# A window-attention block and a deformable convolution on one core: attention's scores and outputs ahead of a slot's sample matmuls, the rare path as a loop of nine passes, turned samples copied by ScalarE

## The chip, the cores and the metric

The kernel runs on one core of a Trainium2 chip. The metric is the device time of one execution in microseconds (us). Everything is computed in float32. The engines are TensorE (PE in the profile; PEld is its weight load), VectorE (DVE), ScalarE (ACT), GpSimd (POOL) and SyncE (SP), which issues nearly all transfers. Each engine takes its instructions strictly in program order and waits on semaphores.

## The reference, cut to what matters

The input is `x`, 16 images of 128 channels and 56x56 pixels. Layer 0 is a block with window attention, layer 1 a modulated deformable 3x3 convolution (8 groups of 16 channels, 9 taps, so 72 samples for each pixel) of one of a few upsampled maps.

```
x = x + dwconv3x3(x, pos_w, pos_b)
y = layernorm(x); q, k, v = y @ qkv_w + qkv_b           # 49 windows of 8x8 pixels
idx = top_k(mean(q) . mean(k), 4)                       # 4 windows of keys for each window
o = softmax(q . k[idx] * SCALE) @ v[idx]                # 4 heads of 32
x = x + (o + dwconv5x5(v, lepe_w)) @ wo_w + wo_b
x = x + gelu(layernorm(x) @ mlp_w1 + mlp_b1) @ mlp_w2 + mlp_b2
...
g = 1 + sigmoid(relu(w_atten . mean(x)))
f = relu(w_off . concat(relu(w_fsm . (x * g)), 2 * feat_up))
off, mask = conv3x3(f, w_offmask) + b_offmask           # 72 dy, 72 dx, 72 mask logits
val = bilinear(feat_up, position + off) * sigmoid(mask) # 4 corners for each of 72 samples
out = relu(w_dcn . val + b_dcn) + x
```

## The kernel before

**Two images at once.** The main loop is software pipelined over images. While layer 0 of image i is computed (`xi` in the code, by the functions `x_slot`, `x_first`, `x_rest`), layer 1 of image i-1 is computed as well (`di`). One round has NT = 28 tiles of two output rows, and each tile has Q = 9 slots, so a round has 252 slots, numbered n = 9 t + q. Fifteen rounds work on two images; before them stands a round with layer 0 alone, and after them one with layer 1 alone. What a slot issues on each engine is written out by hand in the `body` function of that engine; there is no scheduler.

**Layer 1 in a slot.** `windows` (L1025) is 32 small PE matmuls that interpolate eight samples for each pixel along x, from the map piece `fx` and the hat functions `hats`, into one of two PSUM tensors `windows0/1`. `weigh` (L1573) on DVE multiplies the result by the row weights. PE may write slot n only when `weigh` of slot n-2 is done (semaphore `window_weighted`). POOL adds the rows in `add_rows` (L687, L689, L692). In slots q = 5, 6, 7, 8 and 0 PE also turns one or two blocks of finished samples of the tile before (`turn_samples`, L999) into spare columns of the same PSUM tensor, and `copy_samples` (L1562, on DVE right behind `weigh`) copies them to `valt`, 128x256, in q = 0 128x128. `windows` of slot n+2 waits for that copy as well. `deform` (L1036, 9 matmuls, q = 5) consumes `valt`; ScalarE's `relu` (L1279) reads its result. `offsets` (L983, 9 matmuls) stands in q = 0, `turn_columns` (L988) in q = 2, `sum_outside` (L993) in q = 3.

**Attention in slots.** Each of the 49 windows of pixels w has its steps one slot apart, and a new window starts every three slots, from slot A0 = 59 on: slot 0 `scores` on PE (L902); slot 1 `maxes` on DVE (L1489) and `exps` on ACT (L1183); slot 2 `turn` on PE (L911), at the slot's end; slot 3 `copy_turned` on ACT (L1190); slot 4 `pv` on PE (L926); slot 5 `scale_heads` on DVE (L1494, L1496). There are two score banks, so `scores` of window w waits for `scale_heads` of window w-2, which DVE does one slot earlier (semaphore `heads_scaled`). Since 59 leaves 5 when divided by 9, `scores` always stands in q = 2, 5, 8, `pv` in q = 0, 3, 6, and `turn` and `scale_heads` in q = 1, 4, 7. Attention takes slots 59 to 210.

**The 5x5 convolution** on v (`lepe`, L1507 and L1510) is 25 DVE operations for each of seven bands, two or three in each of the 12 slots before a band's end; between them lie 9 slots with the band's output projection and its two-layer network (`post`, steps k = 0 to 8; the Gelu with its table loads is step 7 on ACT, the last matmul step 8 on PE, L956). In the first 27 slots DVE does the 3x3 convolution instead (L1460).

**The rare path.** `general` on POOL runs once a tile, tests a flag and branches over the code at L708 when no sample of the tile lies outside the rows that the fast path holds. Otherwise it recomputes the tile's samples: nine passes, written out one after the other, of 32 gathers (L759), a wait, and four additions and products. In this data one tile of 448 takes it.

The order on PE within a slot is in `body` of the PE program:

```
if di is not None:
    windows(di, t, q)
    ... turn_samples(bi, bt, p, hb[n % 2])
if xi is not None:
    x_first(xi, n)          # pv, then scores
```

behind which come `offsets`, `turn_columns`, `sum_outside`, `deform` and `x_rest` (the projections, `post`, and last `turn`).

Of the kernel before, what the change touches and what calls it, by code (L numbers as in the profile page):

```python
# [8 lines left out]
U32 = mybir.dt.uint32  # L9
ALU = mybir.AluOpType  # L10
ACT = mybir.ActivationFunctionType
# [3 lines left out]
NIMG = B  # L15
# [135 lines left out]
def build(nc, a, out):  # L151
# [9 lines left out]
    with ExitStack() as ctx:  # L161
# [93 lines left out]
        gix = sb("gix", [128, S, 2, 2], U32)  # L255
        gw = sb("gw", [128, S, 2, 2])
        gbuf = sb("gbuf", [128, 8, 2, 2, CG])

        s_w = sem("weights_loaded")
        s_src = sem("small_maps_loaded")  # L260
# [402 lines left out]
        def _(pool):  # L663
# [38 lines left out]
            def general(i, t):  # L702
# [5 lines left out]
                with pool.If(f > 0):  # L708
# [43 lines left out]
                    pool.drain()  # L752
                    pool.tensor_tensor(gw[:, :, 1], gw[:, :, 1], lx, ALU.mult)
                    pool.drain()
                    for n in range(S // 8):
                        for s in range(8):
                            for x in range(2):
                                for y in range(2):
                                    pool.indirect_dma_start(  # L759
                                        gbuf[:, s, x, y], None, fmap,  # L760
                                        bass.IndirectOffsetOnAxis(ap=gix[:, 8 * n + s, x, y:y + 1], axis=0)
                                    ).then_inc(s_fb, 16)
                        pool.wait_ge(s_fb, 32 * 16)
                        hold(pool, "pool")
                        pool.inc_swdge_sem([s_fb], [32 * 16], mode="sub")
                        g = gbuf[:].rearrange("p s x y c -> p (s x y) c")
                        pool.tensor_tensor(g, g, gw[:, 8 * n:8 * n + 8].rearrange("p s x y -> p (s x y)").unsqueeze(2)
                                           .to_broadcast([128, 32, CG]), ALU.mult)
                        pool.drain()
                        pool.tensor_tensor(gbuf[:, :, 0], gbuf[:, :, 0], gbuf[:, :, 1], ALU.add)  # L770
                        pool.drain()
                        pool.tensor_tensor(val[t % 2][:, 8 * n * CG:8 * (n + 1) * CG].rearrange("p (s c) -> p s c", c=CG),
                                           gbuf[:, :, 0, 0], gbuf[:, :, 0, 1], ALU.add)
                        pool.drain()
                pool.drain().then_inc(s_vok, 1)  # L775

# [35 lines left out]
        def _(pe):  # L812
# [254 lines left out]
            def body(xi, di):  # L1067
                for t in range(NT):
                    fi, ft = tile_of(di, xi, t + 2)
                    pi, pt_ = before(di, t, 2)  # L1070
                    for q in range(Q):
                        n = t * Q + q
                        if di is not None:
                            windows(di, t, q)
                            bi, bt, p = pair_of(di, t, q)
                            if bi is not None:
                                turn_samples(bi, bt, p, hb[n % 2])
                        if xi is not None:
                            x_first(xi, n)
                        if fi is not None and q == OM:  # L1080
                            offsets(fi, ft)
                        if fi is not None and q == PXT:
                            turn_columns(fi, ft)
                        if fi is not None and q == PXT + 1:
                            sum_outside(fi, ft)
                        if pi is not None and q == WD:
                            deform(pi, pt_)
                        if xi is not None:
                            x_rest(xi, n)
# [16 lines left out]
        def _(act):  # L1106
# [164 lines left out]
            def row_hats(i, t):  # L1271
                v = wy[t % 2][:].rearrange("p s r -> p (s r)")
                act.wait_ge(s_rab, cnt(i, NT, t + 1))
                act.activation(v, v, ACT.Relu, scale=-1.0, bias=1.0).then_inc(s_wh, 1)

            def relu(i, t):
                act.wait_ge(s_do, cnt(i, NT, t + 1))
                wait(act, s_fin, cnt(i, NT, t - 1))
                act.activation(rt[t % 2][:], bm[:, 216:344], ACT.Relu, bias=col(BD)).then_inc(s_rt, 1)  # L1279
# [22 lines left out]
            def body(xi, di):  # L1302
                for t in range(NT):
                    ni, nt = tile_of(di, xi, t + 1)
                    fi, ft = tile_of(di, xi, t + 2)
                    pi, pt_ = before(di, t, 2)
                    for q in range(Q):
                        hi, hg = group_of(di, xi, t * NG + q // CPG + 1)
                        if hi is not None:
                            column_distances(hi, hg, q % CPG)  # L1310
                        if fi is not None and q == PXT - 1:
                            outside(fi, ft)
                        if fi is not None and q == PXT:
                            copy_columns(fi, ft)
                        if ni is not None and q == WYH:
                            row_sizes(ni, nt)
                        if fi is not None and q == PXT + 1:
                            masks(fi, ft, 0)
                        if pi is not None and q == WD:
                            relu(pi, pt_)  # L1320
                        if ni is not None and q == WYH:
                            row_hats(ni, nt)
                        if fi is not None and q == PXT - 1:
                            outside_sum(fi, ft)
                        if xi is not None:
                            x_slot(xi, t * Q + q)
                        if fi is not None and q in (PXT + 1, PXT + 2):
                            masks(fi, ft, q - PXT)
                        if hi is not None:
                            column_hats(hi, hg, q % CPG)  # L1330
# [4 lines left out]
            with act.Fori(2, NIMG) as i:  # L1335
                body((i, 0), (i, -1))
            body(None, NIMG - 1)
            for t in range(NT - 2, NT):
                relu(NIMG - 1, t)

        @block.vector
        def _(dve):
# [214 lines left out]
            def copy_samples(i, t, p, bank):  # L1557

                dve.wait_ge(s_vt, cnt(i, NP * NT, NP * t + p + 1))
                wait(dve, s_do, cnt(i, NT, t - 1))  # L1560
                k = min(2, KK - 2 * p)
                dve.tensor_copy(valt[t % 2][:, 2 * p:2 * p + k, :], bank[:, 0:k, SPARE:SPARE + 128]).then_inc(s_ve, 1)  # L1562
# [31 lines left out]
            def body(xi, di):  # L1594
                for t in range(NT):
                    fi, ft = tile_of(di, xi, t + 2)
                    for q in range(Q):
# [3 lines left out]
                        if di is not None:  # L1601
                            bi, bt, p = pair_of(di, t, q)
                            if bi is not None:
                                dve.wait_ge(s_vt, cnt(bi, NP * NT, NP * bt + p + 1))
                            weigh(di, t, q)
                            if bi is not None:
                                copy_samples(bi, bt, p, hb[n % 2])
                        if xi is not None:
                            w = step_of(n, 5)
                            if w is not None:  # L1610
# [14 lines left out]
            for t, p in LAST_PAIRS:  # L1625
                copy_samples(NIMG - 1, t, p, hb[p % 2])


# [36 lines left out]
```

## Time and profile before

| | |
|---|---|
| median of three runs | 13466.48 us (13452.15 to 13472.7) |
| profiled execution, its own time | 13485.3 us |
| its span, first to last instruction | 13483.5 us |
| PE busy / weight load busy | 10597.7 us (79%) / 7976.9 us (59%) |
| DVE busy | 8469.6 us (63%) |
| ACT busy | 8472.9 us (63%) |
| POOL busy | 6730.6 us (50%) |
| mean granted PE clock | 0.916 of full speed |

No engine is busy all the time. Set-up takes some 270 us and the first round, with layer 0 alone, ends near 837 us, where the first `weigh` starts. Then the rounds are even. A busy time in the table mixes stretches in which different engines set the pace, so the order of work inside a slot has to be read from the timeline.

### The profile page before, as it was taken

To read this page: it belongs to the slowest core of one execution; us is meant where nothing else is said; L and a number is where in the kernel's file an instruction comes from. 1 tells how busy PE (TensorE), PEld (TensorE's weight loads), DVE (VectorE), ACT (ScalarE), POOL (GpSimd) and SP (SyncE) were. 2 spreads that over 40 slices of the span, in tenths; PEclk is the share of its full clock that TensorE was granted. 3 is DMA by queue.
4 is the path that set the end of the run, shared out by engine and by line. 5 is a ranking of instruction groups with operands and counts; after the bars stand their busy time and mean duration, and the time that the engine had idled before them with its cause. 6 is when DMAs were issued, how large, how long until landed. Compare 5 with 4: busy or idle time off the path is not lost.

```text
span 13483.5 us, 498781 instructions
## 1 busy us (share of the span) xinstructions
PE 10597.7 (79%) x187900; PEld 7976.9 (59%) x187900; DVE 8469.6 (63%) x13829; ACT 8472.9 (63%) x17364; POOL 6730.6 (50%) x6167
## 2 busy tenths in 40 slices
PE   3678888888888888888888888888888888832888
PEld 2346666666666666666666666666666666622666
DVE  6456666666766666676666766666666766622654
ACT  1346666666666666666666666666666666632676
POOL 0034554545455554545455454545545454566467
PEclk8779999999999999999999999999999999976998
DMA  4234454544444454544445454444444444421454
GB/s 130 56 85 121 115 123 116 121 112 121 120 113 122 118 120 109 122 119 115 120 119 121 111 122 118 116 120 121 119 113 121 117 117 121 117 63 39 111 129 109
DMA packets 1847031, 1516.80 MB, mean 112 GB/s; under 512 B 1006688, under 2 KB 1381984, under 8 KB 1841568
## 3 DMA queue, kind: packets, MB, share of 16 engines
q1 hardware_dynamic: 1834468, 1474.31, 44.0%
q8 instruction: 1549, 25.38, 0.8%
q14 instruction: 1798, 14.73, 0.4%
q0 software_dynamic: 9216, 2.38, 0.2%
HBM read 1297.68 MB, written 178.25 MB: 109 GB/s over the span
## 4 chain that ended last, share of the span: by engine, by line
issue 43%; POOLq 25%; PE 11%; POOL 9%; DVE 3%; ACT 3%; DVEq 2%; SPq 2%; DMA 1%; ACTq 0%
POOLq L688 14%; POOLq L690 8%; POOL gbuf L759 2%; POOL wy L679 2%; PE windows L1025 2%; PE bank_small L983 2%; PE bank_small L1036 2%; POOL val L692 1%; POOL xb L699 1%; DVE bank_post L1510 1%; POOLq L705 1%; POOL prod L687 1%; POOL pxy L668 1%; PE bank_scores L902 1%; PE windows L999 1%
## 5 line engine op out<-in xcount | busy, mean ns | idle before, releaser
L1573 DVE TENSOR_TENSOR prod<-windows,wy 128x640 f32<-128x640 f32 x4032 | 3302.2, 821 | 2803.9 <-PE windows L999 1967.4
L687 POOL TENSOR_TENSOR prod<-prod 128x768 f32<-128x768 f32 x1344 | 2452.3, 1825 | 3743.8 <-DVE prod L1573 3736.9
L1025 PEld LDWEIGHTS windows<-fx,hats 64*64 64x64 f32 x129024 | 2629.4, 137 | 1561.6 <-issue 1477.8
L1025 PE MATMUL windows<-fx,hats 64*64 64x80 f32 x129024 | 3278.2, 241 | 341.6 <-issue 118.6
L1234 ACT ACTIVATE hats<-hats,cst 128x512 f32<-128x512 f32 x4032 | 2868.0, 711 | 93.7 <-DMA hats<-sample_columns 59.4
L1238 ACT ACTIVATE hats<-hats 128x512 f32<-128x512 f32 x4032 | 2511.7, 623 | 21.3
L1510 DVE SCALAR_TENSOR_TENSOR bank_post<-xpad,lepw,bank_post 128x448 f32<-128x448 f32 x2688 | 1851.0, 689 | 231.4 <-issue 13.2
L983 PE MATMUL bank_small<-wom,ofp 128*128 128x216 f32 x8064 | 1636.6, 359 | 0.0
L689 POOL TENSOR_TENSOR prod<-prod 128x384 f32<-128x384 f32 x1344 | 1470.7, 1094 | 198.0 <-issue 7.1
L983 PEld LDWEIGHTS bank_small<-wom,ofp 128*128 128x128 f32 x8064 | 1513.3, 199 | 33.4 <-issue 2.7
L692 POOL TENSOR_TENSOR val<-prod 128x384 f32<-128x384 f32 x1344 | 1386.2, 1031 | 269.6 <-issue 230.9
L1183 ACT ACTIVATE pr<-bank_scores,nmx 128x256 f32<-128x256 f32 x1568 | 655.8, 469 | 1267.2 <-DVE nmx L1489 1267.0
L668 POOL TENSOR_SCALAR pxy<-pxy 128x72 f32<-128x72 f32 x448 | 176.6, 394 | 2295.5 <-issue 1388.2
L902 PE MATMUL bank_scores<-ksel,qbd 128*128 128x256 f32 x3136 | 944.7, 428 | 354.8 <-DVE ob L1496 254.2
L911 PE MATMUL bank_scores<-cst,pr 128*128 128x128 f32 x3136 | 532.8, 296 | 861.4 <-ACT pr L1183 861.2
L1036 PE MATMUL bank_small<-valt,wdcn 128*128 128x128 f32 x8064 | 1081.5, 294 | 38.7 <-DVE flag L1555 36.7
L1036 PEld LDWEIGHTS bank_small<-valt,wdcn 128*128 128x128 f32 x8064 | 1066.5, 210 | 63.7 <-issue 42.6
L911 PEld LDWEIGHTS bank_scores<-cst,pr 128*128 128x128 f32 x3136 | 379.7, 149 | 1100.6 <-ACT pr L1183 938.5
L999 PE MATMUL windows<-cst,val 128*128 128x128 f32 x4032 | 961.8, 312 | 45.8 <-POOLq L775 42.1
L902 PEld LDWEIGHTS bank_scores<-ksel,qbd 128*128 128x128 f32 x3136 | 592.1, 210 | 491.7 <-issue 427.5
L1562 DVE COPY valt<-windows 128x256 f32<-128x256 f32 (+1 forms) x2240 | 867.3, 387 | 11.0 <-PE windows L999 11.0
L1279 ACT ACTIVATE rt<-bank_small,cols 128x128 f32<-128x128 f32 x448 | 163.9, 366 | 1127.7 <-PE bank_small L1036 1127.6
(193 smaller groups left out, 12943.8 us busy)
## 6 DMA issues: line engine op xcount, KB each, us to landing
hats<-sample_columns SPq DMA_DIRECT2D x2688, 336.0 KB
ksel<-k_windows SPq DMA_DIRECT2D x3136, 32.0 KB
vsel<-v_windows SPq DMA_DIRECT2D x3136, 32.0 KB
fx<-map_columns SPq DMA_DIRECT2D x64, 420.0 KB
xpad<-in_x SPq DMA_DIRECT2D x17, 1568.0 KB, 11.4
q_windows<-qb SPq DMA_DIRECT2D x112, 224.0 KB, 2.7
k_windows<-kb SPq DMA_DIRECT2D x112, 224.0 KB, 3.0
v_windows<-vb SPq DMA_DIRECT2D x112, 224.0 KB, 3.2
```

The source lines that it names most:

```text
L687: pool.tensor_tensor(v[:, :, 0:n], v[:, :, 0:n], v[:, :, n:2 * n], ALU.add)
L688: pool.drain()
L689: pool.tensor_tensor(v[:, :, 0], v[:, :, 0], v[:, :, 1], ALU.add)
L692: pool.tensor_tensor(val[t % 2][:, g * GS * CG:(g + 1) * GS * CG].rearrange("p (s c) -> p s c", c=CG), v[:, :, 0], v[:, :, 2 if n == 3 els ...
L902: mm = pe.matmul(bank_of(w)[:, h * 256:(h + 1) * 256], qbd[:, j, 2 * h:2 * h + 2, :].rearrange("p h q -> p (h q)"), ksel[s][:], start=True ...
L983: mm = pe.matmul(bm[:, 0:3 * S], ofp[:, at:at + TP], wom[:, k, :], start=(k == 0), stop=(k == KK - 1))
L1025: last[h] = pe.matmul(o[m], hat[:, m], fx[XP * h:XP * h + XP, g, row:row + WR, :].rearrange("p r c -> p (r c)"), start=True, stop=True)
L1036: mm = pe.matmul(bm[:, 216:344], wdcn[:, k, :], valt[t % 2][:, k, :], start=(k == 0), stop=(k == KK - 1))
L1234: act.activation(chunk(n, c), chunk(n, c), ACT.Abs, bias=const("xneg")).then_inc(s_cab, 1)
L1238: act.activation(chunk(n, c), chunk(n, c), ACT.Relu, scale=-1.0, bias=1.0).then_inc(s_hat, 1)
L1510: dve.scalar_tensor_tensor(out=olv, in0=v, scalar=lepw[:, k:k + 1], in1=olv, op0=ALU.mult, op1=ALU.add)
L1573: dve.tensor_tensor(o, x, w.unsqueeze(3).to_broadcast([128, 2, CP * WR, CG]), ALU.mult).then_inc(s_wm, 1)
```

## The change

There are three edits. First, in the PE program `x_first` (that is `pv` and `scores`) moves from behind `windows` and `turn_samples` of the slot to ahead of them. Second, `copy_samples` moves from DVE to ACT: there it stands behind ACT's attention and projection work of the slot and ahead of `column_hats`, and it waits for `weigh` of its slot (`window_weighted`). Third, the nine passes of the rare path become a loop: each pass first copies its indices and weights to the fixed tensors `gin` and `gwn`, and its sum goes to `gsum` and from there to `val`.

```
-                    for n in range(S // 8):
+                    with pool.Fori(0, S // 8) as n:
+                        pool.tensor_copy(gin..., gix...[:, bass.ds(n * 32, 32)])
+                        pool.tensor_copy(gwn..., gw...[:, bass.ds(n * 32, 32)])
+                        pool.drain()
...
-                                        bass.IndirectOffsetOnAxis(ap=gix[:, 8 * n + s, x, y:y + 1], axis=0)
+                                        bass.IndirectOffsetOnAxis(ap=gin[:, s, x, y:y + 1], axis=0)
...
-                        pool.tensor_tensor(val[t % 2][...], gbuf[:, :, 0, 0], gbuf[:, :, 0, 1], ALU.add)
+                        pool.tensor_tensor(gsum[:], gbuf[:, :, 0, 0], gbuf[:, :, 0, 1], ALU.add)
+                        pool.drain()
+                        pool.tensor_copy(val[t % 2][:, bass.ds(n * (8 * CG), 8 * CG)], gsum...)
...
+                        if xi is not None:
+                            x_first(xi, n)
                         if di is not None:
                             windows(di, t, q)
                             bi, bt, p = pair_of(di, t, q)
                             if bi is not None:
                                 turn_samples(bi, bt, p, hb[n % 2])
-                        if xi is not None:
-                            x_first(xi, n)
...
+            def copy_samples(i, t, p, bank):
+                act.wait_ge(s_vt, cnt(i, NP * NT, NP * t + p + 1))
+                wait(act, s_do, cnt(i, NT, t - 1))
+                k = min(2, KK - 2 * p)
+                act.activation(valt[t % 2][:, 2 * p:2 * p + k, :], bank[:, 0:k, SPARE:SPARE + 128],
+                               ACT.Copy).then_inc(s_ve, 1)
...
                         if xi is not None:
                             x_slot(xi, t * Q + q)
+                        if bi is not None:
+                            act.wait_ge(s_wm, cnt(di, NT * Q, t * Q + q + 1))
+                            copy_samples(bi, bt, p, hb[(t * Q + q) % 2])
...
                             weigh(di, t, q)
-                            if bi is not None:
-                                copy_samples(bi, bt, p, hb[n % 2])
```

On PE, in a tile of the attention stretch, slots q = 5 and 6 stand like this in the kernel before (L1025 is `windows`, L999 `turn_samples`, L902 `scores`, L1036 `deform`, L926 `pv`):

```order
L1025 MATMUL windows<-fx,hats 64x80 x16
L999 MATMUL windows<-cst,val 128x128 x2
L902 MATMUL bank_scores<-ksel,qbd 128x256 x2
L1036 MATMUL bank_small<-valt,wdcn 128x128 x9
L1025 MATMUL windows<-fx,hats 64x80 x16
L999 MATMUL windows<-cst,val 128x128 x2
L926 MATMUL bank_scores<-pt,vsel 32x64 x8
L926 MATMUL bank_scores<-pt,cst 32x64 x8
```

The same two slots on PE in the changed kernel, whose line numbers differ (L1036 is now `windows`, L1010 `turn_samples`, L913 `scores`, L1047 `deform`, L937 `pv`):

```order
L913 MATMUL bank_scores<-ksel,qbd 128x256 x2
L1036 MATMUL windows<-fx,hats 64x80 x16
L1010 MATMUL windows<-cst,val 128x128 x2
L1047 MATMUL bank_small<-valt,wdcn 128x128 x9
L937 MATMUL bank_scores<-pt,vsel 32x64 x8
L937 MATMUL bank_scores<-pt,cst 32x64 x8
L1036 MATMUL windows<-fx,hats 64x80 x16
L1010 MATMUL windows<-cst,val 128x128 x2
```

`scores` now stands ahead of the first `windows`, and `pv` between `deform` and the second.

On ACT, the same two slots in the changed kernel (L1298 is `relu`, L1201 `copy_turned`, L1292 the new copy, L1249 and L1245 the hats, L1194 `exps`); in the kernel before the two rows of L1292 are not there and the rest stands the same:

```order
L1298 ACTIVATE rt<-bank_small,cols 128x128 [waits tile_finished,deform_matmul]
L1201 ACTIVATE pt<-bank_scores 128x512 [waits pv_ready,probs_turned]
L1292 ACTIVATE valt<-windows 128x256 [waits deform_matmul,samples_turned,window_weighted]
L1249 ACTIVATE hats<-hats 128x512 [waits column_distances_ready]
L1245 ACTIVATE hats<-hats,cst 128x512 [waits columns_spread0]
L1194 ACTIVATE pr<-bank_scores,nmx 128x256 [waits probs_turned,max_ready]
L1194 ACTIVATE pr<-bank_scores,nmx 128x256
L1292 ACTIVATE valt<-windows 128x256 [waits deform_matmul,samples_turned,window_weighted]
```

`copy_turned`, which `pv` needs, stands behind `relu`, which needs `deform`, in both kernels.

## Rows read from the trace of the kernel before

**Rows 1.** Busy by stretch, ten rounds: us, PE, PEld, DVE, ACT, POOL, clock, DMA.
```profile
3957.00:11759.00 7802.00, 6489.64 (x117080) 4910.62 (x117080) 5174.97 (x8561) 5252.39 (x10800) 4030.32 (x3640) 0.94 0.48 118
```

**Rows 2.** Waits, same stretch: waiter, line, whom; total us, times, longest.
```profile
PE bank_scores L911 <- ACT pr L1183: 270.9, 211, 4.5
PE bank_scores L926 <- ACT pt L1190: 166.7, 160, 1.4
PE bank_scores L902 <- DVE ob L1496: 155.6, 230, 1.2
...
DVE prod L1573 <- PE windows L999: 944.7, 668, 11.1
DVE prod L1573 <- PE windows L1025: 473.2, 505, 3.6
```

**Rows 3.** PE's timeline, slots q = 5 to 8: start, us, line, [idle before].
```profile
6583.25 1.10 PE L902 MATMUL bank_scores<-ksel,qbd 128*128 128x256 f32 x4
6584.19 2.17 PE L1036 MATMUL bank_small<-valt,wdcn 128*128 128x128 f32 x18
6586.29 0.78 PE L1025 MATMUL windows<-fx,hats 64*64 64x80 f32 x32
6587.00 0.44 PE L999 MATMUL windows<-cst,val 128*128 128x128 f32 x2
6587.39 0.43 PE L926 MATMUL bank_scores<-pt,vsel 128*32 128x64 f32 x16
...
6592.92 1.10 PE L902 MATMUL bank_scores<-ksel,qbd 128*128 128x256 f32 x4 [0.85 <-DVE ob L1496]
```

**Rows 4.** DVE's timeline, slots q = 7 and 8 of that tile.
```profile
6590.86 0.82 DVE L1573 TENSOR_TENSOR prod<-windows,wy 128x640 f32<-128x640 f32 x1
6591.59 0.41 DVE L1562 COPY valt<-windows 128x256 f32<-128x256 f32 x1
6591.92 0.55 DVE L1494 RECIPROCAL rinv<-bank_scores 128x64 f32<-128x64 f32 x1
6592.55 0.22 DVE L1496 TENSOR_TENSOR ob<-bank_scores,rinv 128x64 f32<-128x64 f32 x1
6592.86 1.45 DVE L1510 SCALAR_TENSOR_TENSOR bank_post<-xpad,lepw,bank_post 128x448 f32<-128x448 f32 x2
6594.23 0.82 DVE L1573 TENSOR_TENSOR prod<-windows,wy 128x640 f32<-128x640 f32 x1
```

**Rows 5.** ACT's timeline, that tile: slot q = 2, then slot q = 5.
```profile
6577.49 0.27 ACT L1243 ACTIVATE pxs<-bank_small 72x128 f32<-72x128 f32 x1 [0.58 <-PE bank_small L988]
6577.80 0.50 ACT L1269 ACTIVATE wy<-wy 128x360 f32<-128x360 f32 x1
...
6578.74 0.58 ACT L1190 ACTIVATE pt<-bank_scores 128x512 f32<-128x512 f32 x1
...
6586.40 0.37 ACT L1279 ACTIVATE rt<-bank_small,cols 128x128 f32<-128x128 f32 x1 [2.50 <-PE bank_small L1036]
6586.66 0.59 ACT L1190 ACTIVATE pt<-bank_scores 128x512 f32<-128x512 f32 x1
```

**Rows 6.** The page's costliest groups: busy us, mean ns, idle before, releaser.
```profile
L1562 DVE COPY valt<-windows 128x256 f32<-128x256 f32 (+1 forms) x2240 | 867.3, 387 | 11.0 <-PE windows L999 11.0
L1183 ACT ACTIVATE pr<-bank_scores,nmx 128x256 f32<-128x256 f32 x1568 | 655.8, 469 | 1267.2 <-DVE nmx L1489 1267.0
```

**Rows 7.** PE's timeline, step 8 of `post`, and the clock of its stretch.
```profile
6638.00 4.84 PE L956 MATMUL bank_post<-hid,w 128*128 128x448 f32 x6 [3.75 <-ACT hid L1208]
6638.00:6642.80 4.80, 4.80 (x7) 2.23 (x8) 0.00 (x0) 3.93 (x7) 0.00 (x0) 0.50 0.58 135
```

**Rows 8.** POOL, whole span: the gathers, and the first operation behind the branch.
```profile
L759 POOL DMA_INDIRECT gbuf<-map_columns,gix x288 | 272.2, 945 | 92.2 <-issue 92.2
L668 POOL TENSOR_SCALAR pxy<-pxy 128x72 f32<-128x72 f32 x448 | 176.6, 394 | 2295.5 <-issue 1388.2
```

More of the change, by code:

```diff
@@ L257, in build @@
         gbuf = sb("gbuf", [128, 8, 2, 2, CG])
+        gin = sb("gin", [128, 8, 2, 2], U32)
+        gwn = sb("gwn", [128, 8, 2, 2])
+        gsum = sb("gsum", [128, 8, CG])
         s_w = sem("weights_loaded")
@@ L754, in general @@
                     pool.drain()
-                    for n in range(S // 8):
+                    with pool.Fori(0, S // 8) as n:
+                        pool.tensor_copy(gin[:].rearrange("p s x y -> p (s x y)"),
+                                         gix[:].rearrange("p s x y -> p (s x y)")[:, bass.ds(n * 32, 32)])
+                        pool.tensor_copy(gwn[:].rearrange("p s x y -> p (s x y)"),
+                                         gw[:].rearrange("p s x y -> p (s x y)")[:, bass.ds(n * 32, 32)])
+                        pool.drain()
                         for s in range(8):
@@ L766, in general @@
                         g = gbuf[:].rearrange("p s x y c -> p (s x y) c")
-                        pool.tensor_tensor(g, g, gw[:, 8 * n:8 * n + 8].rearrange("p s x y -> p (s x y)").unsqueeze(2)
+                        pool.tensor_tensor(g, g, gwn[:].rearrange("p s x y -> p (s x y)").unsqueeze(2)
                                            .to_broadcast([128, 32, CG]), ALU.mult)
@@ L771, in general @@
                         pool.drain()
-                        pool.tensor_tensor(val[t % 2][:, 8 * n * CG:8 * (n + 1) * CG].rearrange("p (s c) -> p s c", c=CG),
-                                           gbuf[:, :, 0, 0], gbuf[:, :, 0, 1], ALU.add)
+                        pool.tensor_tensor(gsum[:], gbuf[:, :, 0, 0], gbuf[:, :, 0, 1], ALU.add)
+                        pool.drain()
+                        pool.tensor_copy(val[t % 2][:, bass.ds(n * (8 * CG), 8 * CG)],
+                                         gsum[:].rearrange("p s c -> p (s c)"))
                         pool.drain()
@@ L1326, in body @@
                             x_slot(xi, t * Q + q)
+                        bi, bt, p = pair_of(di, t, q) if di is not None else (None, None, None)
+                        if bi is not None:
+                            act.wait_ge(s_wm, cnt(di, NT * Q, t * Q + q + 1))
+                            copy_samples(bi, bt, p, hb[(t * Q + q) % 2])
                         if fi is not None and q in (PXT + 1, PXT + 2):
@@ L1337, in _ @@
             body(None, NIMG - 1)
-            for t in range(NT - 2, NT):
-                relu(NIMG - 1, t)
+            for t, p in LAST_PAIRS:
+                copy_samples(NIMG - 1, t, p, hb[p % 2])
+                if p == NP - 1:
+                    relu(NIMG - 1, t)
         @block.vector
@@ L1555, in flags @@
                 dve.tensor_scalar(flag[0:1, t % 4:t % 4 + 1], bm[0:1, 472:473], 0.0, None, ALU.is_gt).then_inc(s_fl, 1)
[L1557 to L1562, printed above, removed]
             def weigh(i, t, q):
@@ L1624, in _ @@
             body(None, NIMG - 1)
-            for t, p in LAST_PAIRS:
-                copy_samples(NIMG - 1, t, p, hb[p % 2])
 def kernel(**inputs):
```

## The prediction

> **What bounds the kernel now.** I read the busy table by stretch first, then the waits, then the timelines of one tile. The ten even rounds take 780.2 us each, PE is busy for 83% of them, DVE for 66%, ACT for 67% and POOL for 52% [rows 1], so no engine alone is the bound: they hand work to each other. The waits say how. DVE waits before `weigh` for PE's sample matmuls, 142 us a round, and PE waits for ACT and DVE before the three attention steps: 27 us a round before `turn`, 17 before `pv`, 16 before `scores` [rows 2]. These waits are short and frequent, so what stands behind each of them in PE's order matters.
>
> The timelines show a tile of a stretch in which DVE also has taps of the 5x5 convolution. There DVE has no gap from `weigh` of q = 7 to `weigh` of q = 8: product 0.73 from start to start, copy 0.33, reciprocal and scaling 0.85 to the result, two taps 1.37 to the next product [rows 4]. PE was a slot ahead: `scores` of q = 8 started 0.15 us after the scaling ended, and it had waited 0.85 us for it [rows 3, 4], with `windows` of q = 8 already done. That order, samples first and attention's waits second, is what lets DVE go on. In this stretch DVE is the bound.
>
> **Part 1, the copy leaves DVE.** It costs DVE 0.33 us in a slot with two blocks [rows 4] and an estimated 0.20 in q = 0, so 1.5 us a tile of nine slots. On ACT I take 0.42 us for it: `exps` reads the same 128x256 from PSUM in 0.47, and DVE's mean is 0.39 [rows 6]. ACT is busy for two thirds, and `column_hats` behind the copy is made three slots ahead, so this lies beside other work. It adds a wait: ACT stands until `weigh` of the slot is done; behind it are the hats and then `copy_turned`. `windows` two slots later waits for the copy as before, with about a slot to spare. Alone this part would gain up to 1.5 us a tile where DVE is the bound.
>
> **Part 2, `pv` and `scores` ahead of the samples.** Here I follow one tile with taps in the new order. Lengths: `scores` 0.94 from start to start, `windows` 0.71 and then the turned samples 0.44 to their end, `deform` 2.10 [rows 3]; `pv` 0.50 (two halves, estimated from the 0.43 of each and their overlap); a signal between engines about 0.08 (an estimate between the 0.04 from `deform`'s end, at 6586.36, to `relu` and the 0.15 above) [rows 3, 5].
> (a) *q = 2, 5, 8.* Count from the end of scaling in the slot before. Now `scores` must run before `windows`: 0.08 + 0.94 + 0.78 + 0.08 = 1.88 us until `weigh` may start, and in q = 5 and 8, with turned samples, 0.08 + 0.94 + 0.71 + 0.44 + 0.08 = 2.25. DVE has only its taps to do, 0.09 + 1.37 = 1.46. It stalls 0.4 + 0.8 + 0.8 = 2.0 us a tile where it stalled for nothing.
> (b) *q = 6.* `pv` needs `copy_turned`, which stands on ACT behind `relu`, which needs `deform` of q = 5 [rows 3, 5]. Before, `windows` of q = 6 ran in that time: it began at 6586.29, `relu` at 6586.40, the copy at 6586.66, `pv` at 6587.39. Now from the start of `weigh` of q = 5: `deform`, begun about 0.2 before, ends at +1.95, `relu` lets the copy start at +2.27, which ends at +2.86, `pv` runs from +2.94 for 0.50, `windows` and samples end at +4.59, `weigh` may start at +4.67. DVE is ready at 0.74 + 1.46 = 2.20, so it stalls 2.5 us.
> (c) *q = 3.* `copy_turned` stands behind the copy of the turned columns, which needs L988 behind `windows` of q = 2, and behind two operations on the row weights; from 6577.49 to its start is 1.25 us, and it takes 0.58 [rows 5]. From the start of `weigh` of q = 2: +0.2 for L988, +1.25, +0.58, +0.08, `pv` 0.50, `windows` 0.78, signal 0.08: 3.4 against DVE's 2.2, a stall of 1.2 us.
> The three stalls make 5.7 us. Less the 1.5 us of part 1 and about 0.2 that DVE stalls there now, a tile with taps becomes 4.0 us longer. The taps stand in 7 x 12 = 84 of the 152 attention slots, 9.3 tiles: +37 us a round.
> In the other 68 slots (7.6 tiles) DVE has slack, but the chain through PE has the same three waits ahead of `windows`. From below, 0: they lie beside what `post` makes PE wait for anyway. From above, 4.0 as with taps. I take 2.7, nearer the upper end, since (b) and (c) are waits of PE itself and don't depend on taps: +20 us a round. In slots 0 to 58 `x_first` is empty; DVE does the 3x3 convolution in 27 of them and I count three tiles of part 1, -4 us.
> A round gains 37 + 20 - 4 = 53 us, fifteen rounds 800 us.
>
> **Part 3, the loop in the rare path.** It runs once, and all engines stand meanwhile. Its 288 gathers take (272.2 + 92.2) / 288 = 1.27 us each [rows 8] in either form. Each pass adds two copies of 32 numbers, one of 128 and two drains; I take 1.3 us, so 12 in all, between 5 and 20. Eight jumps back: the nearest row is the branch over the code, behind which POOL stands 1388.2 / 448 = 3.1 us on the mean [rows 8]; bounds 0 and 6, taken 2.6, so 21 us. The sum is +33, from +5 to +70. The branch over the path now skips about a ninth of the code. That may shorten those 3.1 us, but POOL waits for DVE's products anyway, and I count nothing. The Trainium skill (Runtime: NRT & Kernel Launch, Instruction fetch mechanics) speaks against the loop: a taken branch to code that is not at hand forces a fetch, and unrolled code is preferred. By it the eight jumps cost like the one over the code, 8 x 3.1 = 25 us; it changes the sum by 4 us.
>
> **Sum.** 13485.3 + 800 + 33 = 14318 us for the profiled execution. This lies 19 us above the median of the runs, so the median of the changed kernel should be near 14300 us, 6% slower.
>
> **The rivals.**
> *The copy decides.* If PE, freed from waits by an earlier `pv`, stayed a slot ahead, stalls (a) to (c) would not form, and only part 1 would be left: 1.5 us in 9.3 + 3 tiles, 18 us a round, 15 x 18 = 277 us less, plus 33: 13220. For it: DVE has no gap in the tile with taps, so each operation that leaves counts. Against it: `scores` was seen to wait for the scaling 230 times in 490, though it stood behind `windows` [rows 2]. It decides from the point where the scaling ends more than 2 us before `windows` is due. Chance 8%.
> *The delays are half absorbed.* PE's stalls may merge with waits it has now, which are 780.2 - 649.0 = 131 us a round in all [rows 1]. Then 27 us a round: 13467 + 400 + 33 = 13900. Chance 18%.
> *The clock falls.* After 3.75 us without a matmul in step 8 of `post`, the granted clock was 0.50 (1.2 GHz) and six matmuls took 4.84 us [rows 7]. New gaps of 1 to 2 us could lower it elsewhere. If it were lower by 0.05 of 0.94 [rows 1], the 649 us that PE is busy in a round would grow by 5%, 34 us, fifteen times: 500 more, 14800. Against it: the four matmuls of `scores` took 1.10 us behind a gap of 0.85 as they did behind none [rows 3]. The Trainium skill (TensorE: Matmul & The Clock Gate, HAM oscillation) has this as a rule: idle gaps between bursts make the clock fall again and again. The rows agree for the long gap and not for the short ones. Chance 15%.
> *It cancels.* Stalls and the copy's gain meet within 0.2%, 13440 to 13493. Chance 3%.
>
> **How the numbers follow.** The forecast has 56%. The 2.7 us of the slots without taps, taken from 0 to 4, alone move it by 15 x 7.6 x 2.7 = 308 down and 148 up, to 13990 and 14450; the loop's bounds move it by 28 down and 37 up. The range reaches into the absorbed and the clock case: 13800 to 14700. A measurement of this kernel tells about 0.2% from no change. Faster by more than that: 0.08; within: 0.03; slower: 0.89.
>
> **What would show it.** Right: in rounds of about 833 us, PE's wait before `pv` for L1201 and before `scores` for the scaling grow to several times their 17 and 16 us, DVE's wait before `weigh` for `windows` grows from 142 us by about 50, DVE is busy 867.3 / 16 = 54 us a round less [rows 6] and ACT as much more; before `windows` of q = 6 stands `pv`, which waited about 1 us for `copy_turned`; the rare path takes some 30 us longer. Wrong: if `weigh` of q = 6 starts within 3 us of that of q = 5, (b) is false; if rounds without attention waits are longer too, it is ACT's new wait that delays the hats; if PE's mean clock is under 0.90 in the rounds, the clock case holds.

## The result, and the profile after

| | before | after |
|---|---|---|
| median | 13465.69 us (4 runs) | 14665.61 us (14653.94 to 14686.4, 4 runs) |
| ratio | | 1.089, 95% interval 1.0875 to 1.0913 |
| span of the profiled execution | 13483.5 us | 14660.6 us |
| mean granted PE clock | 0.916 | 0.894 |
| PE, DVE, ACT, POOL busy | 79, 63, 63, 50% | 75, 54, 61, 46% |

The changed kernel is 1200 us or 8.9% slower. The forecast was 14300 us, with a range from 13800 to 14700.

In the kernel after, line numbers are shifted: `windows` is L1036, `turn_samples` L1010, `scores` L913, `turn` L922, `pv` L937, `deform` L1047, the copy L1292 on ACT, `weigh` L1592. First, ten rounds by the busy table (us, then PE, PEld, DVE, ACT, POOL, clock, DMA share, GB/s), to be read against [rows 1], and the waits of the same stretch against [rows 2]:

```profile
3406.00:12032.00 8626.00, 6748.88 (x117082) 5027.82 (x117081) 4807.03 (x7161) 5587.76 (x12201) 4039.96 (x3640) 0.91 0.43 106
```

```profile
PE bank_scores L937 <- ACT pt L1201: 445.1, 350, 1.9
PE bank_scores L913 <- DVE ob L1522: 389.6, 312, 1.6
PE bank_scores L922 <- ACT pr L1194: 298.6, 210, 1.6
...
DVE prod L1592 <- PE windows L1010: 1841.6, 936, 10.5
DVE prod L1592 <- PE windows L1036: 788.9, 679, 3.7
```

A round takes 862.6 us instead of 780.2, 82.4 more. It splits in two: PE is busy 674.9 us instead of 649.0, with the same number of matmuls, which is 25.9 us of slower matmuls; and PE is idle 187.7 us instead of 131.2, which is 56.5 us of waits. Where the trace has the clock at 0.50, PE is busy for 78.2 us of a round before and for 130.1 after. At full speed the 51.9 us more would have been half as long, so 26.0 us of busy time come from the clock, which is the whole growth. PE's waits before `pv` and `scores` grew from 17 and 16 to 45 and 39 us a round, and DVE's wait before `weigh` from 142 to 263.

The tile with taps, on PE (start, us, engine, line, names, [idle before]); it answers to [rows 3]:

```profile
7250.20 1.10 PE L913 MATMUL bank_scores<-ksel,qbd 128*128 128x256 f32 x4 [1.24 <-DVE ob L1522]
...
7254.18 0.43 PE L937 MATMUL bank_scores<-pt,vsel 128*32 128x64 f32 x16 [1.93 <-ACT pt L1201]
...
7258.05 1.12 PE L922 MATMUL bank_scores<-cst,pr 128*128 128x128 f32 x4 [1.03 <-ACT pr L1194]
7260.31 2.04 PE L913 MATMUL bank_scores<-ksel,qbd 128*128 128x256 f32 x4 [1.14 <-DVE ob L1522]
7262.28 1.34 PE L1036 MATMUL windows<-fx,hats 64*64 64x80 f32 x32
7263.56 0.69 PE L1010 MATMUL windows<-cst,val 128*128 128x128 f32 x2
7264.04 2.91 PE L1047 MATMUL bank_small<-valt,wdcn 128*128 128x128 f32 x18
7267.99 0.43 PE L937 MATMUL bank_scores<-pt,vsel 128*32 128x64 f32 x16 [1.04 <-ACT pt L1201]
```

And `weigh` on DVE in the slots q = 2 to 8 of that tile, of which [rows 4] show q = 7 and 8 before:

```profile
7252.11 0.82 DVE L1592 TENSOR_TENSOR prod<-windows,wy 128x640 f32<-128x640 f32 x1 [0.52 <-PE windows L1036]
...
7255.70 0.82 DVE L1592 TENSOR_TENSOR prod<-windows,wy 128x640 f32<-128x640 f32 x1 [1.22 <-PE windows L1036]
...
7258.58 0.82 DVE L1592 TENSOR_TENSOR prod<-windows,wy 128x640 f32<-128x640 f32 x1
...
7264.37 0.83 DVE L1592 TENSOR_TENSOR prod<-windows,wy 128x640 f32<-128x640 f32 x1 [2.62 <-PE windows L1010]
...
7269.94 0.82 DVE L1592 TENSOR_TENSOR prod<-windows,wy 128x640 f32<-128x640 f32 x1 [3.20 <-PE windows L1010]
...
7272.81 0.82 DVE L1592 TENSOR_TENSOR prod<-windows,wy 128x640 f32<-128x640 f32 x1
...
7278.61 0.82 DVE L1592 TENSOR_TENSOR prod<-windows,wy 128x640 f32<-128x640 f32 x1 [1.91 <-PE windows L1010]
```

DVE has a gap wherever the prediction put one: before q = 2, 3, 5, 6 and 8. Together they are 9.5 us, where the prediction had 5.7. `scores` of q = 5 takes 2.04 us where it took 1.10, `windows` 1.34 for 0.78, the turned samples 0.69 for 0.44. The busy table says why, with the clock in the third column from the right:

```profile
7252.20:7254.20 2.00, 0.07 (x4) 0.05 (x5) 1.83 (x3) 1.82 (x5) 1.18 (x1) 1.00 0.22 49
...
7255.60:7256.90 1.30, 1.30 (x36) 1.14 (x34) 1.20 (x2) 0.00 (x0) 1.10 (x2) 0.50 0.98 258
...
7260.20:7264.70 4.50, 4.39 (x42) 3.42 (x43) 1.72 (x4) 0.36 (x1) 0.00 (x0) 0.50 0.14 37
...
7266.00:7267.00 1.00, 0.95 (x9) 0.76 (x7) 0.69 (x1) 0.01 (x1) 1.00 (x1) 1.00 0.86 279
...
7272.20:7273.30 1.10, 1.02 (x4) 0.65 (x4) 1.09 (x2) 1.10 (x4) 0.00 (x0) 0.59 0.23 58
```

The clock fell to its lower level, 1.2 GHz, soon after PE had waited 1.24 us before `scores` of q = 2 and 1.93 us before `pv` of q = 3, with 2.05 us of matmuls between the two waits. It stayed there through the next two waits, 1.03 and 1.14 us, and came back during the 2.91 us of `deform`.

On POOL, the gathers and the first operation behind the branch, to be read against [rows 8] (the second from the answer by lines):

```profile
L768 POOL DMA_INDIRECT gbuf<-map_columns,gin x288: 938/944/1189, 13104.1 to 13511.4; - x144
L672 POOL TENSOR_SCALAR pxy<-pxy 128x72 f32<-128x72 f32 x448 | 198.8, 444 | 1081.0 <-DVE pxy L1577 930.4 <-issue 150.6
```

From the branch to the end of the rare path it is 417.4 us before and 428.9 after. The idle time put down to issue behind the branch fell from 1388.2 to 150.6 us. From the branch to the next instruction it was 2.8 us at the median of the 448 times before, and 0.4 after.

### The profile page after: what moved, and what is told of

It is laid out like the page before. It is cut to its first block, busy times and chain, and to the rows that moved or that the text cites. A ratio compares the mean times of both kernels' runs of the same rounds, so it can differ in the third digit from the quotient of the medians.

```text
span 14660.6 us, 500856 instructions
## 1 busy us (share of the span) xinstructions
PE 10958.6 (75%) x187900; PEld 8130.5 (55%) x187900; DVE 7870.5 (54%) x11589; ACT 8998.4 (61%) x19604; POOL 6754.0 (46%) x6194
## 4 chain that ended last, share of the span: by engine, by line
PE 39%; issue 23%; DVEq 9%; POOLq 8%; DVE 8%; ACT 8%; POOL 4%; ACTq 1%; DMA 1%; SPq 1%
PE windows L1036 10%; PE bank_small L994 6%; POOLq L692 4%; PE bank_small L1047 4%; PE bank_scores L913 4%; DVEq L1485 3%; PE windows L1010 3%; DVEq L1521 3%; POOLq L694 2%; PE bank_scores L937 2%; PE bank_post L967 2%; DVE bank_post L1536 2%; DVEq L1535 2%; POOL gbuf L768 2%; DVE prod L1592 2%
## 5 line engine op out<-in xcount | busy, mean ns | idle before, releaser
L1592 DVE TENSOR_TENSOR prod<-windows,wy 128x640 f32<-128x640 f32 x4032 | 3306.5, 822 | 4578.4 <-PE windows L1010 3305.9
L1036 PE MATMUL windows<-fx,hats 64*64 64x80 f32 x129024 | 3433.9, 249 | 317.7 <-ACT valt L1292 154.0
L1036 PEld LDWEIGHTS windows<-fx,hats 64*64 64x64 f32 x129024 | 2768.5, 144 | 1543.8 <-issue 1440.5
L1245 ACT ACTIVATE hats<-hats,cst 128x512 f32<-128x512 f32 x4032 | 2885.2, 716 | 41.7 <-issue 41.7
L1249 ACT ACTIVATE hats<-hats 128x512 f32<-128x512 f32 x4032 | 2521.1, 625 | 0.5
L913 PE MATMUL bank_scores<-ksel,qbd 128*128 128x256 f32 x3136 | 1056.0, 469 | 731.0 <-DVE ob L1522 603.5
L696 POOL TENSOR_TENSOR val<-prod 128x384 f32<-128x384 f32 x1344 | 1445.3, 1075 | 268.3 <-issue 237.6
L1194 ACT ACTIVATE pr<-bank_scores,nmx 128x256 f32<-128x256 f32 x1568 | 657.0, 470 | 1337.1 <-DVE nmx L1515 1337.1
L1292 ACT ACTIVATE valt<-windows 128x256 f32<-128x256 f32 (+1 forms) x2240 | 806.3, 360 | 742.5 <-DVE prod L1592 694.8
L922 PE MATMUL bank_scores<-cst,pr 128*128 128x128 f32 x3136 | 539.9, 299 | 915.7 <-ACT pr L1194 915.7
L913 PEld LDWEIGHTS bank_scores<-ksel,qbd 128*128 128x128 f32 x3136 | 629.4, 222 | 934.5 <-issue 868.5
L1298 ACT ACTIVATE rt<-bank_small,cols 128x128 f32<-128x128 f32 x448 | 163.7, 365 | 1479.3 <-PE bank_small L1047 1479.2
L1047 PE MATMUL bank_small<-valt,wdcn 128*128 128x128 f32 x8064 | 1044.0, 287 | 32.6 <-DVE flag L1581 31.8
L1047 PEld LDWEIGHTS bank_small<-valt,wdcn 128*128 128x128 f32 x8064 | 1011.6, 204 | 47.3 <-issue 45.0
L922 PEld LDWEIGHTS bank_scores<-cst,pr 128*128 128x128 f32 x3136 | 381.2, 150 | 1139.7 <-ACT pr L1194 991.4
L1010 PE MATMUL windows<-cst,val 128*128 128x128 f32 x4032 | 997.8, 323 | 4.2 <-issue 1.6
L937 PE MATMUL bank_scores<-pt,vsel 128*32 128x64 f32 x12544 | 367.6, 239 | 668.3 <-ACT pt L1201 668.3
```

What stands on the lines that cost most here:

```text
L696: pool.tensor_tensor(val[t % 2][:, g * GS * CG:(g + 1) * GS * CG].rearrange("p (s c) -> p s c", c=CG), v[:, :, 0], v[:, :, 2 if n == 3 els ...
L913: mm = pe.matmul(bank_of(w)[:, h * 256:(h + 1) * 256], qbd[:, j, 2 * h:2 * h + 2, :].rearrange("p h q -> p (h q)"), ksel[s][:], start=True ...
L1010: mm = pe.transpose(bank[:, k % 2, SPARE:SPARE + 128], val[t % 2][:, k * 128:(k + 1) * 128], ident)
L1036: last[h] = pe.matmul(o[m], hat[:, m], fx[XP * h:XP * h + XP, g, row:row + WR, :].rearrange("p r c -> p (r c)"), start=True, stop=True)
L1047: mm = pe.matmul(bm[:, 216:344], wdcn[:, k, :], valt[t % 2][:, k, :], start=(k == 0), stop=(k == KK - 1))
L1245: act.activation(chunk(n, c), chunk(n, c), ACT.Abs, bias=const("xneg")).then_inc(s_cab, 1)
```

## The experiments

All ratios are against runs of the kernel before on the same chip. In the code cuts, what stands behind # is a note of this text.

**e1_order: the first edit alone.**

```
+                        if xi is not None:
+                            x_first(xi, n)
                         if di is not None:
                             windows(di, t, q)
...
-                        if xi is not None:
-                            x_first(xi, n)
```

> Only the first edit: pv and scores ahead of the sample matmuls on PE; the copy stays on DVE, the rare path stays unrolled. Theory 'order' (PE's sample matmuls now stand behind attention's waits, and that is the whole loss): at least as slow as the changed kernel, 14650 to 15000 us, since DVE also keeps the 1.5 us of copies a tile. Rival 'ScalarE' (the new wait of ScalarE for weigh delays hats and copies, the order costs little): within 150 us of the kernel before, 13450 to 13600.

Measured: 15041.16 us, ratio 1.117 (1.1155 to 1.1193). Ten of its rounds:

```profile
3479.00:12317.00 8838.00, 6857.43 (x117082) 5123.41 (x117081) 5214.87 (x8561) 5252.42 (x10800) 4020.47 (x3640) 0.90 0.42 104
```

It loses 1572 us, more than the whole change and a little more than its theory's upper end of 15000. 'ScalarE' falls: nothing of the loss needs the copy on ACT. A round is 103.6 us longer: 198.1 us idle (66.9 more) and 685.7 busy (36.8 more).

**e2_copy: the second edit alone.**

```
+                        if bi is not None:
+                            act.wait_ge(s_wm, cnt(di, NT * Q, t * Q + q + 1))
+                            copy_samples(bi, bt, p, hb[(t * Q + q) % 2])      # ScalarE
...
                             weigh(di, t, q)
-                            if bi is not None:
-                                copy_samples(bi, bt, p, hb[n % 2])            # VectorE
```

> Only the second edit: copy_samples on ScalarE. Theory 'order': faster than before by 100 to 280 us, 13190 to 13370, since DVE is relieved of 1.5 us a tile where it sets the pace. Rival 'ScalarE': slower by several hundred us, 14000 and more. The changed kernel's last round (layer 1 alone) was 49 us shorter than before; if that comes from the copy, it is seen here too, if it comes from the shorter branch over the rare path, it is not.

Measured: 13330.4 us, ratio 0.990 (0.9887 to 0.9921), 139 us faster. The copies on ACT and what they wait for:

```profile
L1281 ACT ACTIVATE valt<-windows 128x256 f32<-128x256 f32 (+1 forms) x2240 | 806.7, 360 | 468.5 <-DVE prod L1581 411.0 <-PE windows L999 54.3
```

ACT stands 411 us for `weigh` in the whole kernel, and the kernel is faster all the same: the rounds are 771 us. From the first to the last `weigh` of the last round (layer 1 alone) the kernel before takes 514.7 us, the changed kernel 465.2 and this one 504.2, so most of what the changed kernel saved there is not the copy's.

**e3_loop: the third edit alone.**

```
-                    for n in range(S // 8):
+                    with pool.Fori(0, S // 8) as n:
...
```

> Only the third edit: the rare path as a loop. The changed kernel's trace has the rare path at 428.9 us from branch to end against 417.4, and the branch over it at 0.4 against 2.8 us. If PowerL's branch is covered by waits: 13465 + 12 = 13477 us. If it is exposed in the last round (28 tiles of 2.4 us) and at tile starts: 50 to 100 us less than before, 13370 to 13420.

('PowerL' is a slip for POOL.) Measured: 13385.99 us, ratio 0.994 (0.992 to 0.9963), 83 us faster. POOL's first operation behind the branch:

```profile
L672 POOL TENSOR_SCALAR pxy<-pxy 128x72 f32<-128x72 f32 x448 | 190.2, 425 | 1147.6 <-DVE pxy L1562 1043.5 <-issue 91.9 <-DVE flag L1566 12.2
```

The last round takes 456.2 us instead of 514.7, 58 less, and the others 2.5 less at the median. In the last round of the kernel before, the branch is seen to be exposed; its waits there:

```profile
POOL pxy L668 <- issue: 92.3, 25, 5.2
...
ACT pxy L1258 <- POOL pxy L668: 42.7, 19, 3.4
...
DVE prod L1573 <- POOL val L692: 38.1, 25, 3.1
...
PE windows L999 <- POOLq L775: 27.0, 16, 2.5
```

POOL's late `samples_checked` holds PE's `turn_samples`, and its late masks and sums hold DVE. The sum is right: 58 in the last round and 14 times 2.5 in the others, less the 11.5 that the rare path takes longer, make 82. In rounds with attention so little of the branch is left; that it lies beside other waits there is argued, not tried.

**e4_scores and e5_pv: the first edit in two halves.** In the first, only `scores` goes ahead of `windows`, in the second only `pv`.

> The kernel before with scores alone ahead of windows; pv stays behind it. Stall (a) of the prediction alone: 2.0 us a tile in 16.9 tiles is 34 us a round, 13980 us; with matmuls at the 1.2 GHz level behind the longer gap up to 60 us a round, 14370. Rival (the whole loss sits with pv, scores cost nothing): 13420 to 13520.

> The kernel before with pv alone ahead of windows; scores stay behind it. Stalls (b) and (c): 3.7 us a tile in 16.9 tiles is 62 us a round, 14400 us; between 14200 and 14700. Rival (the loss sits with scores): 13420 to 13600. If the two halves are independent, their losses add up to the 1572 us of both.

Measured: 14273.9 us, ratio 1.060 (1.0578 to 1.0627) for `scores`, and 14294.51 us, ratio 1.062 (1.0595 to 1.0638) for `pv`. Ten rounds of each, and the wait that each step has:

```profile
3335.00:11664.00 8329.00, 6718.51 (x117084) 5008.17 (x117083) 5215.79 (x8561) 5254.44 (x10801) 4024.51 (x3642) 0.92 0.44 110
PE bank_scores L902 <- DVE ob L1500: 481.9, 385, 2.0
PE bank_scores L926 <- ACT pt L1194: 166.8, 160, 1.4
```

```profile
3334.00:11677.00 8343.00, 6690.94 (x117083) 5077.45 (x117082) 5186.54 (x8561) 5251.27 (x10801) 4032.73 (x3641) 0.91 0.44 110
PE bank_scores L926 <- ACT pt L1194: 432.7, 343, 2.1
PE bank_scores L902 <- DVE ob L1500: 128.4, 203, 1.2
```

Each half lengthens its own wait and not the other's, which stays (166.8 us for 166.7) or gets a little shorter (128.4 for 155.6). The losses of 799 and 820 us add up to 1619, those of both together were 1572: they are nearly independent. The loss with `scores` ahead lies between the 13980 of the stall alone and the 14370 with slow matmuls, as forecast. A round is 52.7 us longer with `scores` ahead and 54.1 with `pv`: idle time grew by 29.8 and 34.0 us, busy time by 22.9 and 20.1. Against the forecast idle time, 34 for (a) fits, and 62 for (b) and (c) was nearly double of what is seen.

**e6_filler and e9_filler4: does the clock matter?** Both are the changed kernel with small matmuls ahead of every `pv` and `scores`; their results aren't used. They wait for what `windows` of the slot waits for, so `pv` and `scores` behind them now do as well, which is a second change beside the filled gap.

```
+                    for _ in range(8):        # 4 in e9_filler4
+                        pe.matmul(hb[(t * Q + q) % 2][:, 0, 448:512], ident, const("ident")[:, 0:64],
+                                  start=True, stop=True)
...
+                        if xi is not None and di is not None and (
+                                step_of(n, 4) is not None or step_of(n, 0) is not None):
+                            filler(di, t, q)  # waits for what windows(di, t, q) waits for
                         if xi is not None:
                             x_first(xi, n)
```

> The changed kernel with eight small matmuls (128x128 weights, 64 columns, about 0.8 us in all) on PE ahead of every pv and every scores, into spare columns of the PSUM tensor that the slot's samples will go to; their result is not used. They wait for what windows waits for anyway and fill part of the idle time. Theory 'clock' (a good part of the loss over the forecast 53 us a round comes from matmuls at the 1.2 GHz level): granted clock in the rounds back to 0.94 or more and 14250 to 14500 us. Theory 'order alone': the stalls are the same and the fillers cost where PE had no wait, 14700 to 14900 us.

> The changed kernel with four small matmuls ahead of every pv and every scores instead of eight. Eight took 1.90 us in the trace, longer than the gap of 1.14 before scores, so they cost more than they could give; four take about 0.9 us. In the trace with eight, scores took 1.10 us again where they take 2.04 in the changed kernel. Theory 'clock': the gap before scores and pv no longer lowers the clock, granted clock at 0.93 or more, 14300 to 14600 us. Theory 'the clock follows the stall and costs little': 14670 to 15000.

Measured: 15738.04 us, ratio 1.169 (1.1666 to 1.1705) with eight, and 15148.77 us, ratio 1.124 (1.1225 to 1.1263) with four. Both are slower than the changed kernel, and than every time that either theory allowed. With eight, on PE at the same slots as above:

```profile
7788.54 0.66 PE L922 MATMUL bank_scores<-cst,pr 128*128 128x128 f32 x4 [1.61 <-ACT pr L1208]
7789.03 1.90 PE L1059 MATMUL windows<-cst 128*128 128x64 f32 x16
7790.80 1.10 PE L913 MATMUL bank_scores<-ksel,qbd 128*128 128x256 f32 x4
7791.83 0.78 PE L1036 MATMUL windows<-fx,hats 64*64 64x80 f32 x32
...
7789.00:7793.00 4.00, 4.00 (x58) 3.52 (x57) 3.00 (x7) 2.04 (x5) 0.00 (x0) 1.00 0.24 56
```

Here the clock is at full speed, and `scores` and `windows` take 1.10 and 0.78 us as in the kernel before. So it was the clock that made them 2.04 and 1.34 us, and with the gaps filled it stays up: over ten rounds it is 0.95, for 0.91 in the changed kernel. That was the clock theory's sign; its time was missed because eight fillers take 1.90 us and not the 0.8 that was expected, more than the gap of 1.14, 98 times a round. Four (1.00 us) come where there was no gap too, and don't always hold the clock: in q = 8 of the same tile `scores` took 1.91 us again. As a price of the clock these two runs decide nothing; as a repair they fail.

**e10_turned: does `pv` wait for what stands ahead of `copy_turned`?** The changed kernel, with `copy_turned` first in ACT's slot.

```
+                        if xi is not None:
+                            x_turned(xi, t * Q + q)      # copy_turned
                         hi, hg = group_of(di, xi, t * NG + q // CPG + 1)
                         if hi is not None:
                             column_distances(hi, hg, q % CPG)
```

> The changed kernel with copy_turned as the first thing ScalarE does in its slot, ahead of relu (which waits for deform), of the copy of the turned columns and of the row weights. If stalls (b) and (c) come from copy_turned standing behind these, as the prediction says, PE's wait before pv (445 us in ten rounds) nearly goes, the step from weigh of q = 5 to weigh of q = 6 falls from 5.6 to about 4.3 us, and the time to 14100 to 14450. If pv waits for something else: 14600 to 14700.

Measured: 14268.39 us, ratio 1.060 (1.0575 to 1.0623), 397 us less than the changed kernel. PE's longest waits in ten rounds:

```profile
PE bank_scores L913 <- DVE ob L1526: 408.1, 330, 1.6
PE bank_scores L922 <- ACT pr L1194: 379.4, 210, 2.4
PE bank_post L967 <- ACT hid L1219: 195.2, 60, 4.3
PE windows L1036 <- ACT valt L1292: 90.6, 117, 2.1
```

The wait before `pv` for ACT fell from 445 to 14 us; a part of it moved to `turn` (379 for 299). In tile t = 13, at the median of the rounds, the step from `weigh` of q = 2 to that of q = 3 is 2.3 us for 3.6, and it was 2.3 in the kernel before: stall (c) was the order on ACT. From q = 5 to 6 it is 4.4 for 5.5, but it was 3.05 before: about half of (b) was the order on ACT. In the one such tile that was looked at, `deform` (2.85 us for 2.17), `pv` and `windows` run one behind the other without a wait. The rounds also show that idle and busy time can be read apart:

```profile
3323.00:11658.00 8335.00, 6785.05 (x117082) 5073.39 (x117081) 4794.55 (x7160) 5587.89 (x12200) 4039.82 (x3641) 0.90 0.44 110
```

Against the changed kernel a round has 32.7 us less idle and 3.6 us more busy time, 29.1 less in all, though the clock is lower.

**e7_copy_loop and e11_best: without the first edit.** e7 has the second and third edits; e11 also has `copy_turned` first on ACT.

> The second and third edits without the first: copies on ScalarE and the loop, attention behind the samples as before. Alone they gave 139 and 83 us; added up: 13247 us. If both shorten the same waits of the last round, less: 13290.

> As the run with both later edits, and copy_turned first in ScalarE's slot. PE waits 17 us a round for it before pv. If that wait is on the path: 50 to 200 us less than without, 13050 to 13200. If scores and turn only wait longer instead: the same within 30 us.

Measured: 13265.17 us, ratio 0.985 (0.9834 to 0.9867), and 13305.77 us, ratio 0.988 (0.9866 to 0.9899). Ten rounds of e7:

```profile
3140.00:10819.00 7679.00, 6455.58 (x117082) 4877.40 (x117081) 4763.61 (x7161) 5587.06 (x12201) 4052.59 (x3640) 0.95 0.49 119
PE bank_scores L913 <- DVE ob L1522: 120.3, 242, 0.5
```

The two edits nearly add up (139 + 83 = 222, measured 196), and e7 beats both kernels. Moving `copy_turned` ahead, which gave 397 us in the changed kernel, costs 40 here, and neither forecast (50 to 200 less, or the same within 30) held. In ten rounds PE's wait for ACT before `pv` goes from 169.9 us to none, but its wait before `turn` grows from 238.1 to 364.5. That the second comes from the hats and `exps` standing behind ACT's wait for PE's `turn` is argued and was not tried by itself.

## Why the prediction was right, and where it was short

**The direction and the mechanism were right.** The first edit is the whole loss and more (e1_order), by PE's sample matmuls standing behind attention's waits. The two halves are nearly independent (e4, e5).

**The stalls came out near as idle time, and partly by luck.** The forecast was +53 us a round; PE's idle time grew by 56.5, the round by 82.4. Without part 1 the forecast is 53 + 18 = 71, and e1_order has 66.9; the copy and the loop then took 10.4 us of idle time, where part 1 was to take 18. The two misses partly cancel. e5_pv shows (b) and (c) over all tiles at 34.0 us of idle time, about half of the 62 that they would make if every tile were like the one worked out. By slots (the steps from `weigh` to `weigh`, mean of ten rounds) the 84 with taps became 54.7 us longer and not 37, the other 68 of attention 26.1 and not 20, and the rest 1.3 us longer and not 4 shorter. So a tile with taps became 5.9 us longer where 4.0 were forecast.

Of its three stalls, (c) was to put 3.4 us from `weigh` of q = 2 to that of q = 3 (its terms add up to 3.47); it was 7255.70 - 7252.11 = 3.59. For (b) `pv` was to wait about 1 us for `copy_turned` in q = 6; it waited 1.04. But `weigh` of q = 6 was to follow that of q = 5 after 4.67 us and followed after 5.57, with 0.74 us of the excess in `deform`, which took 2.91 for 2.17. For (a) the step from `weigh` of q = 4 to q = 5 was to be 0.74 + 0.85 + 2.25 = 3.84; it was 5.79, and from q = 7 to q = 8 it was 5.80.

**The step that was mis-sized is the clock.** The sum took all lengths from rows at full speed. Of the excess of 1.95 us in (a), 1.75 is matmuls at 1.2 GHz: `scores` 0.94, `windows` 0.56 and the turned samples 0.25 us longer. Over a round it is the 25.9 us by which PE's busy time grew. They make 25.9 x 15 = 389 us of the 1200, for which the sum had no term; the distance between 14300 and 14666 is 366, since smaller misses stand on both sides, the idle time 3.5 us a round above and the last round 49 us below. The prediction had this as a rival on its own ('The clock falls', 34 us a round), and its sign for it, a mean clock under 0.90 in the rounds, was not met: it was 0.91. It set against it that `scores` took 1.10 us behind a gap of 0.85. That row was about one gap. The same tile of the kernel before has longer ones, at full speed throughout (the last line is of the busy table):

```profile
6579.47 0.43 PE L926 MATMUL bank_scores<-pt,vsel 128*32 128x64 f32 x16 [1.36 <-ACT pt L1190]
...
6590.33 0.66 PE L911 MATMUL bank_scores<-cst,pr 128*128 128x128 f32 x4 [1.20 <-ACT pr L1183]
...
6574.90:6602.00 27.10, 22.19 (x494) 18.01 (x493) 24.36 (x43) 18.61 (x43) 13.41 (x12) 1.00 0.47 128
```

In the new order there is a gap before `scores`, before `pv`, before `turn` and before `scores` again, each of 1 to 2 us with 1 to 3 us of matmuls between, and the clock did fall. Over ten rounds it fell 29.4 times a round instead of 18.9. The Trainium skill (TensorE: Matmul & The Clock Gate, HAM oscillation) has it that idle gaps between bursts make the clock fall again and again; its example has longer waits than these. The trace agrees for the short gaps here, with a granted clock of 0.50 at 7255.60 and still at 7264.70, though each gap by itself is shorter than the 3.75 us of [rows 7]. It should have been a term of the sum and not a rival to it: the two don't exclude each other.

**The copy** was to be free on ACT, at 0.42 us: it takes 0.36 on the mean and gives 139 us alone, half of the 277 of the first rival. With the first edit in place it gives more: from e1_order to the changed kernel a round gets 21.2 us shorter by copy and loop, where part 1 was to give 18, and the whole kernel 15041 - 14666 = 375. What the loop has of that was not run; alone it gave 83. That the copy gives more there because reciprocal and maxima stand behind it on DVE, and PE waits for both at once, is argued.

**The loop** was to cost 33 us. It cost 11.5, and 12 stood for the added operations alone. The eight jumps back, taken at 2.6 us each, are about 0.16 each in the trace, from the branch to the next instruction, 1.3 us together. What was counted as nothing, the shorter branch over the path, brought more than that: 58 us in the last round alone. The error was to judge it from the even rounds, where POOL has slack, and not from the last round, where it has none. By the Trainium skill (Runtime: NRT & Kernel Launch, Instruction fetch mechanics) unrolled code is to be preferred; here the loop wins, since the code is passed over 447 times and executed once. The reason that it gives, a fetch when the target is not at hand, fits 2.8 us over nine passes of code against 0.4 and 0.16 over one; the fetch itself is seen in no trace here.

**The rivals.** 'The copy decides' and 'It cancels' fell with e1. 'Half absorbed' fell: idle time grew by 56.5 us a round, not by half of the 53.

**The signs.** PE's waits before `pv` and `scores` grew to 2.7 and 2.5 times what they were, short of 'several times'. DVE's wait for `windows` was to grow by 50 us a round and grew by 121, since the round is 82 us longer and DVE has 37 us less to do. DVE's busy time was to fall by 54 us and ACT's to rise as much; it was 37 and 34. One reason is that the 54 adds up the copies' full lengths, 0.41 us each, while the next operation starts 0.33 us after a copy does [rows 4].

## What to carry to other kernels

In an in-order queue, put work whose inputs are ready ahead of work that has to wait, even when the waiting work is on the longer chain: moving `scores` and `pv` by one place cost 6% each. When an edit adds gaps to PE, price the matmuls around them at the slow clock as well, as a term of the sum: 25.9 of 82.4 us a round here. A rarely executed block can cost time at every pass over it, 2.8 us for the long form here and 0.4 for the short one, so keep it short, and look for the stretch where the engine that jumps has no slack.

## What the runs showed of the hardware

The granted clock fell to 0.50 behind gaps of 1.24 and 1.93 us close together. A single gap of 1.04 (before `pv` at 7267.99, behind `deform`) left the halves of `pv` at 0.43 us. The next fall in the same tile came right behind a gap of 1.48, with 2.8 us of matmuls between the two: the clock is 0.59 from 7272.20 to 7273.30, and `scores` of q = 8 takes 2.05 us. But the kernel before has gaps of 1.20 and 0.85 with 1.74 us of matmuls between them, and of 1.36 before, at 1.00 throughout. A reader should look at all the gaps of a stretch and not at the longest one. Where the line lies was not tried.

A branch over nine passes of gather code took 2.8 us at the median, and 7.7 or more in one time of a hundred; over one pass it took 0.4. The eight backward jumps over one pass took 0.16 to 0.19 us each.

A filler matmul in float32 with 128x128 weights and only 64 columns takes about 0.24 us (eight in 1.90, four in 1.00). The matmuls of `deform`, with the same weights' size and 128 columns, take as much at full speed (nine in 2.10), so the columns don't set the price. That the weight load does is likely, but was not tried.
